# Moving an expert's gate and up products ahead of the preceding expert's down product, on TensorE and ScalarE

## The reference, cut to what matters

```python
xe = buf[:E * CAP].reshape(E, CAP, H)                 # 32 experts x 512 slots x 256
gu = jnp.einsum('ech,eoh->eco', xe, gate_up_proj)     # gate and up, 128 features each
g, u = (gu[..., :I], gu[..., I:])
g = jnp.minimum(g, LIMIT)
u = jnp.clip(u, -LIMIT, LIMIT)
h = jax.nn.silu(g) * u
ye = jnp.einsum('eci,ehi->ech', h, down_proj)         # back to 256 features
```

## Time and profile before

| what | value |
|---|---|
| timed runs, median of 3 | 3159.44 us |
| profiled execution, span from first to last instruction | 3342.4 us |
| TensorE busy | 3124.5 us (93%) |
| VectorE busy | 2625.2 us (79%) |
| ScalarE busy | 1965.3 us (59%) |
| GpSimd busy | 2101.7 us (63%) |
| mean granted clock of TensorE | 0.969 |
| first matmul of `run_experts` | 747.6 us from the start |
| last copy of `run_experts` begins | 958.4 us from the start |
| first matmul of `attend` | 964.9 us from the start |

### The profile page before, as it was taken

How to read it: one execution, slowest core, us unless ns; L and a number is a source line. 1 busy time by engine, 2 the same in 40 slices (tenths; PEclk the granted TensorE clock), 3 DMA queues, 4 the chain that set the end, 5 groups by cost and what they waited for, 6 DMA issues and landing times.

```text
span 3342.4 us, 53910 instructions
## 1 busy us (share of the span) xinstructions
PE 3124.5 (93%) x13443; PEld 1609.9 (48%) x13444; DVE 2625.2 (79%) x2773; ACT 1965.3 (59%) x3797; POOL 2101.7 (63%) x2148
## 2 busy tenths in 40 slices
PE   7965659999979999999999999999999999999998
PEld 3433323445544555555555555455555555555554
DVE  8600013433359999999999999999999999999995
ACT  4500003203447777777777777677777777777775
POOL 4877771001126777777777777667777777777776
PEclk9987769999989999999999999999999999999999
DMA  8810017776658988879899888898888889888987
GB/s 315 326 66 23 17 42 283 252 178 209 229 155 227 227 226 215 220 202 222 225 223 225 215 217 204 210 253 221 225 220 217 214 209 221 225 223 218 219 204 182
DMA packets 318996, 685.52 MB, mean 205 GB/s; under 512 B 120749, under 2 KB 170680, under 8 KB 318544
## 3 DMA queue, kind: packets, MB, share of 16 engines
q1 hardware_dynamic: 289744, 626.48, 71.1%
q0 software_dynamic: 29184, 58.22, 5.4%
HBM read 198.37 MB, written 159.51 MB: 107 GB/s over the span
## 4 chain that ended last, share of the span: by engine, by line
PE 64%; DMA 2%; SPq 1%; DVE 1%; issue 1%; POOL 1%; ACT 0%; POOLq 0%; ACTq 0%
PE at_ps L1110 26%; PE at_ps L1142 25%; PE at_ps L1157 8%; PE at_ps L1123 5%; DMA at_moved<-at_blocks 1%; SPq L934 1%; DVE at_half_max L1239 1%; DVE at_blocks L1256 1%; DMA out<-ahead_acc 0%; POOL at_moved L1052 0%; POOL ahead_acc L1067 0%; ACT at_prob L1193 0%; DMA ahead_acc<-base 0%; SPq L783 0%; POOL ahead_acc L1044 0%
## 5 line engine op out<-in xcount | busy, mean ns | idle before, releaser
L1193 ACT ACTIVATE at_prob<-at_ps,at_neg_max 128x1024 f32<-128x1024 f32 x1024 | 1150.4, 1123 | 323.7 <-DVE at_neg_max L1244 284.5
L1239 DVE TENSOR_REDUCE at_half_max<-at_ps 128x1 f32<-128x1024 f32 x1024 | 1202.2, 1215 | 26.6 <-PE at_ps L1110 25.2
L1256 DVE STREAM_TRANSPOSE at_blocks<-at_prob 128x1792 f32<-128x1792 f32 x512 | 1043.1, 2037 | 5.9 <-DMA at_moved<-at_blocks 3.2
L1052 POOL COPY at_moved<-at_blocks 32x1792 f32<-32x1792 f32 x512 | 858.2, 1676 | 159.2 <-DVE at_blocks L1256 61.0
L1110 PE MATMUL at_ps<-ahead_k_hl,ahead_q_hh 128*128 128x512 f32 x2048 | 854.1, 417 | 22.9 <-ACT at_prob L1193 16.2
L1142 PE MATMUL at_ps<-at_moved,at_v 128*64 128x512 f32 x3584 | 863.2, 595 | 6.9 <-DMA at_moved<-at_blocks 6.9
L1110 PE MATMUL at_ps<-ahead_k_hl,ahead_q_ll 128*128 128x512 f32 x2048 | 809.4, 395 | 0.0
L1067 POOL TENSOR_TENSOR ahead_acc<-ahead_acc,at_scaled 128x256 f32<-128x256 f32 x512 | 376.5, 735 | 228.0 <-ACT at_scaled L1205 105.6
L1110 PEld LDWEIGHTS at_ps<-ahead_k_hl,ahead_q_hh 128*128 128x128 f32 x2048 | 388.6, 190 | 96.9 <-ACT at_prob L1193 24.2
L1142 PEld LDWEIGHTS at_ps<-at_moved,at_v 128*64 128x64 f32 x3584 | 262.5, 138 | 354.5 <-issue 299.6
L1205 ACT ACTIVATE at_scaled<-at_ps,at_inv 128x256 f32<-128x256 f32 x512 | 242.9, 474 | 316.2 <-PE at_ps L1157 263.0
(11 more groups left out here) (112 smaller groups left out, 2783.7 us busy)
## 6 DMA issues: line engine op xcount, KB each, us to landing
at_moved<-at_blocks SPq DMA_DIRECT2D x1536, 224.0 KB
ahead_k_hl<-k_parts SPq DMA_DIRECT2D x64, 512.0 KB, 8.2
ahead_q_hh<-q_parts SPq DMA_DIRECT2D x128, 256.0 KB, 4.3
ahead_q_ll<-q_parts SPq DMA_DIRECT2D x128, 256.0 KB, 6.1
xbuf<-pr_zeros SPq DMA_DIRECT2D x32, 512.0 KB, 3.9
q_parts<-pr_part_hi SPq DMA_DIRECT2D x64, 256.0 KB
q_parts<-pr_part_lo SPq DMA_DIRECT2D x64, 256.0 KB
k_parts<-pr_part_hi SPq DMA_DIRECT2D x64, 256.0 KB
```

The lines of the kernel that those rows point to most:

```text
L1052: nc.gpsimd.tensor_copy(moved[r * 32:(r + 1) * 32, parity, r, :, :, :], blocks[r * 32:(r + 1) * 32, parity, r, :, :, :]).then_inc(diag_don ...
L1193: nc.scalar.activation(prob[:, i % 2, half * 1024:(half + 1) * 1024], ps[:, banks[0]:banks[1], :].rearrange("p b c -> p (b c)"), ACT.Exp, ...
L1239: nc.vector.tensor_reduce(half_max[:, i % 2, half:half + 1], ps[:, banks[0]:banks[1], :], AX.XY, ALU.max).then_inc(max_step, 1)
L1256: nc.vector.transpose(blocks[:, parity, :, j, :, :].rearrange("p c t k -> p t c k"), prob[:, (s["s"] - 1) % 2, 0:MOVED * P].rearrange("p ( ...
```

## The change

TensorE's loop becomes turn(n), gate_up(n), down(n-1), and ScalarE's becomes copy of turn(n), silu(n), copy of down(n-1). The two experts ahead of the loop are followed by down(0), and only down(31) stands behind the loop. The other streams, the buffers, the semaphores, their waits and the instructions themselves are as before.

```diff
@@ ScalarE
-            for q in range(2):
-                turn(0, q)
-                silu(0, q)
+            turn(0, 0)
+            silu(0, 0)
+            turn(0, 1)
+            silu(0, 1)
+            down(0, 0)
 
             def both(i):
-                for q in range(2):
-                    turn(i, q)
-                    down(i - 1, q)
-                    silu(i, q)
+                turn(i, 0)
+                silu(i, 0)
+                down(i - 1, 1)
+                turn(i, 1)
+                silu(i, 1)
+                down(i, 0)
...
-            for q in range(2):
-                down(E // 2 - 1, q)
+            down(E // 2 - 1, 1)
@@ TensorE
-            for q in range(2):
-                turn(0, q)
-                gate_up(0, q)
+            turn(0, 0)
+            gate_up(0, 0)
+            turn(0, 1)
+            gate_up(0, 1)
+            down(0, 0)
+
             def both(i):
-                for q in range(2):
-                    turn(i, q)
-                    down(i - 1, q)
-                    gate_up(i, q)
+                turn(i, 0)
+                gate_up(i, 0)
+                down(i - 1, 1)
+                turn(i, 1)
+                gate_up(i, 1)
+                down(i, 0)
...
-            for q in range(2):
-                down(E // 2 - 1, q)
+            down(E // 2 - 1, 1)
```

## The result

| | before | after |
|---|---|---|
| timed median | 3156.76 us (4 runs, 3153.70 to 3163.32) | 3196.28 us (4 runs, 3192.32 to 3201.47) |
| ratio of after to before, 95% interval | | 1.0126 [1.0108, 1.0144] |
| profiled span | 3342.4 us | 3195.1 us |
| first matmul of `attend` to the end of the span | 2377.5 us | 2377.9 us |
| line 697 (700 after), first start to last start, 31 experts | 196.0 us | 232.6 us |

What follows compares the result with a forecast made beforehand. TensorE's chain was taken to pace the expert loop (25.19 of 25.30 us busy). 30 experts at 7.56 us, 226.8, less 189.8, give +37.0 us on 3159.44: 3196.4 us forecast, range 3185 to 3212.

Steps and rivals of the forecast that it cites:

- Instructions and their order: Expert loop: no instruction added or removed; TensorE has nothing to do after turn(n) until ScalarE has copied its result.
- The period: Expert loop, time per expert: 7.56 us in place of 6.325, over 30 experts +37.0 us.
- T: The moment gate_up(n-1) ends on TensorE, from which the steps of the new period are counted.
- the bare copy: ScalarE's copy of turn(n), formerly covered by a down product, leaves TensorE idle some 1.2 to 1.6 us per expert.
- the queue on ScalarE: The turn's copy waits for the down product's copy, 0.17 us per expert; rival without it: +31.9 us, 3191 us.
- The ends of the block and the rest: Start and end of the expert block keep their order and gain or lose nothing; attention stays as long as before.
- The clock: TensorE's granted clock in the expert loop stays at 1.00 despite pauses of some 1.5 us in every 7.56; no cost.
- the 7%: Chance of the rival that TensorE's clock falls in the new pauses: 92 us on top, 3288 us.
- The loads: SP's loads of expert weights: margin grows from 0.25 to 3.6 us, which gives nothing back.
- The rival built on them: Late loads pace the old loop in timed runs, so the change gains: 22 us less, 3137 us; chance 3%.
- The span of 3342.4 us: Profiled span before, 183 us above the timed median of 3159.44; which block holds the excess was left open.
- the 35 of a shrink in proportion: Alternative to adding the loop's 37.0 us unscaled to the timed median: 35 us if everything shrank in proportion.

Runs made afterwards that it cites:

- TensorE alone: Against the kernel before, only TensorE took the new order and ScalarE kept the old one; 3192.08 us, ratio 1.0111.
- in halves: The full change, with the copy of the turned slots split into two halves so that gate and up begin on the first; 3183.01 us, ratio 1.0081.
- ScalarE alone reordered: Against the kernel before, only ScalarE took the new order and TensorE kept the old one; 3268.13 us, ratio 1.0350.
- with the copy in halves as well: Against the kernel before, ScalarE only in the new order, and the copy of the turned slots split into two halves; 3208.49 us, ratio 1.0162.
- With 4.9 us and a later issue: Each expert's slots loaded twice, the second time into an unread buffer: 3172.25 us in the old order, 3195.43 us in the new.

## Why the prediction was right, point by point

- *Instructions and their order.* Nothing added or removed; on TensorE the only thing that changed its length in the loop is the wait ahead of gate and up, 1.14 to 1.30 us in all 30 experts (1.2 to 1.6 forecast). Right.
- *The period.* 7.56 us were forecast, 7.55 came. The mechanism is the one forecast. The steps in it were off by up to 0.13 us and made up for each other, so that the sum came out to 0.01 us is luck: the copy of the down product at T + 2.00 (1.93 forecast), the turn's copy at T + 2.92 (2.98), gate and up at T + 3.98 in this expert (4.02), 3.54 us of gate and up. The spacing of two ScalarE copies was 0.92 us. I had taken 1.05 from the pair in the earlier trace rows, but there the second copy was still waiting for its product (783.31 + 1.89 = 785.20, and it began at 785.24), so that row wasn't a spacing. From the start of that copy to gate and up were 1.06 to 1.15 where I had 1.04.
- *What makes it up.* Both parts were shown by doing them alone or in part: the bare copy (TensorE alone, +33.4 us of loop; in halves, -14.1) and the queue on ScalarE (3.2 us more in the full change, by the traces; 0.17 x 30 = 5 us had been forecast).
- *The ends of the block and the rest.* The loop gained 36.6 us, attention is as long as before to 0.4 us, and the timed runs moved by 39.5, with an interval of 34 to 45. Right; what lies between 36.6 and 39.5 isn't resolved. From the first matmul of the block to that of `attend` the two profiled executions differ by less, 35.3 us (217.3 before, 252.6 after), as gate and up of expert 0, ahead of the loop and in the same order in both, took 6.77 us in the one and 5.36 in the other.
- *The clock.* Costed at nothing; 1.00 in the loop after. Right, but with less room than the 7% suggest: in this same loop pauses of 1.67 us kept the clock, and of 2.0 to 2.2 us lost it in 27 of 30 experts. The reason given, the busy time of stretches in the earlier trace rows, doesn't separate the two: with ScalarE alone reordered TensorE was busy for 31.79 of 40 us at a clock of 0.83, and with the copy in halves as well for 31.67 at 1.00. In part this was luck.
- *The loads.* They had room afterwards, as forecast. The rival built on them had a step wrong: "its period would be 1.96 + landing + 0.43" takes every expert to wait. Since only every second does, two periods together are bounded by 6.03 + 1.96 + landing + 0.43, and the change would have been a gain from a landing of 6.7 us (estimate: 2 x 7.56 - 8.42), not 5.2. With 4.9 us and a later issue the new order still lost by 23 us.
- *The span of 3342.4 us.* The prediction left open where the 183 us above the timed median lay. They lay in the first block: `run_experts` began at 747.6 us there and at 564.6 in the changed kernel's profile, with the first block's code untouched, and the first block was as short in all seven profiles of the experiments. In the long one VectorE's line 439 and TensorE's shared-expert products waited, partly for nothing that the profile shows. What held them up in that one execution stays open. As the whole excess lay outside the loop, adding the 37 us unscaled was sound; the timed runs, with 34 to 45 us, don't tell 37 from the 35 of a shrink in proportion.

## What to carry to other kernels

In an engine that takes its instructions in order, a product that looks movable may be the cover of a copy: before moving it, look what the engine will wait for in its place, and price that from T, the end of the step before, along both queues. A spot where the same program already runs the new order, such as the last or first round of a loop, gives the steps of the price: here to about a tenth of a us each. And where two engines hand work back and forth, the order on the copying engine should follow the order in which the other will need it: putting the copy that TensorE needs next ahead of silu was worth 0.3% here, with no other edit.

## What the runs showed of the hardware that I had not expected

A recurring pause of 1.67 us in 7.97 left TensorE at 2.4 GHz throughout the loop, and one of 2.0 to 2.2 us cost it half the clock for about four of eight passes in 27 of 30 experts, mean granted clock 0.83: from there 0.5 us of pause cost another 1.7 us of passes. In the three others the same pause cost nothing more; what set them apart stays open.
